# Resident expert weights in a macaron of attention, RWKV and four expert mixtures: per-tile weight transfers replaced by on-chip copies and register-addressed products

## What is computed

```
# glu stage (gated)
gate_logits = x @ Wg + bg
top_vals, top_idx = top_k(gate_logits, 2);  w = softmax(top_vals)
h = einsum('td,edh->eth', xf, W0) + b0          # d = 128, h = 512
g = silu(einsum('td,edh->eth', xf, W1) + b1)
y = einsum('eth,ehd->etd', h * g, W2) + b2
out = sum over the two chosen experts of w * y
# mlp stage (ungated): gelu(x @ W1 + b1) @ W2 + b2 for the two chosen,
# plus a shared gelu(x @ shared_W + shared_b), a layer norm, and the residual
```

## Time and profile before

| | |
|---|---|
| runs, median (lowest to highest) | 1119.5 us (1117.77 to 1120.09), 3 runs |
| profiled execution | 1118.18 us, its span 1116.4 us |
| TensorE busy | 797.7 us (71% of the span), 5220 matmul records |
| VectorE, ScalarE, GpSimd busy | 538.7, 445.3, 433.3 us (48%, 40%, 39%) |
| chain that ended last | PE 58%, DVE 24%, issue 7%, DMA 4%, ACT 3%, POOL 3% |
| DMA traffic | 153.77 MB, mean 138 GB/s |

### The profile page before, as it was taken

How to read it: one execution, slowest core, us unless ns; L and a number is a source line. 1 busy time by engine, 2 the same in 40 slices (tenths; PEclk the granted TensorE clock), 3 DMA queues, 4 the chain that set the end, 5 groups by cost and what they waited for, 6 DMA issues and landing times.

```text
span 1116.4 us, 17251 instructions
## 1 busy us (share of the span) xinstructions
PE 797.7 (71%) x5220; PEld 680.7 (61%) x5220; DVE 538.7 (48%) x1633; ACT 445.3 (40%) x1259; POOL 433.3 (39%) x448
## 2 busy tenths in 40 slices
PE   0579997378989865899974767774177877777750
PEld 0479997267777645798973566664034555666650
DVE  4734444777656537344447521113889543310117
ACT  0045554144445320455550145553087331265540
POOL 1256663022222210565631066663453210466631
PEclk9999999698989985799995579997598885699995
DMA  4559985362513003598954247775000011477752
GB/s 110 131 177 293 291 271 180 95 152 55 124 42 82 2 9 121 179 291 279 276 174 132 94 114 213 211 207 144 1 0 1 1 30 35 136 212 211 210 162 65
DMA packets 79082, 153.77 MB, mean 138 GB/s; under 512 B 11082, under 2 KB 54035, under 8 KB 78992
## 3 DMA queue, kind: packets, MB, share of 16 engines
q1 hardware_dynamic: 69008, 134.03, 40.6%
q0 software_dynamic: 9984, 18.65, 6.1%
HBM read 134.21 MB, written 20.25 MB: 138 GB/s over the span
## 4 chain that ended last, share of the span: by engine, by line
PE 58%; DVE 24%; issue 7%; DMA 4%; ACT 3%; POOL 3%; SPq 1%; another core or an unknown queue 0%; POOLq 0%; ACTq 0%; DVEq 0%
PE bank L521 14%; PE bank L512 12%; PE bank L509 8%; PE bank L945 2%; DVE stats L281 2%; PE bank L528 2%; PE bank L460 2%; PE bank L935 2%; DVE oh_b L623 2%; PE bank L497 2%; DVE sh_tok L675 2%; PE bank L1270 2%; DVE x_tok L675 2%; PE bank L908 1%; PE bank L477 1%
## 5 line engine op out<-in xcount | busy, mean ns | idle before, releaser
L512 PE MATMUL bank<-xt,weights 128*128 128x128 f32 x1248 | 249.8, 283 | 27.5 <-ACT xt L411 16.6
L521 PE MATMUL bank<-hid,weights 128*128 128x128 f32 x1248 | 245.1, 279 | 11.0 <-ACT hid L422 8.2
L348 POOL DMA_INDIRECT xg<-xn_rows,gidx x156 | 153.1, 982 | 238.7 <-DVE gidx L629 129.9
L512 PEld LDWEIGHTS bank<-xt,weights 128*128 128x128 f32 x1248 | 196.5, 199 | 33.9 <-ACT xt L411 20.3
L521 PEld LDWEIGHTS bank<-hid,weights 128*128 128x128 f32 x1248 | 191.1, 194 | 15.3 <-ACT hid L422 9.5
L355 POOL DMA_INDIRECT y_rows<-yo,sidx x156 | 157.1, 1007 | 91.8 <-issue 56.3
L650 DVE SCALAR_TENSOR_TENSOR hid<-bank,weights,act_ring 128x128 f32<-128x128 f32 x312 | 108.9, 349 | 139.5 <-ACT act_ring L422 83.2
L422 ACT ACTIVATE act_ring<-bank,weights 128x128 f32<-128x128 f32 x312 | 115.8, 371 | 111.1 <-PE bank L512 96.5
L657 DVE COPY yo<-bank 128x128 f32<-128x128 f32 x156 | 44.6, 286 | 213.2 <-remote 127.6
L422 ACT ACTIVATE hid<-bank,weights 128x128 f32<-128x128 f32 x312 | 110.6, 372 | 79.8 <-PE bank L521 51.1
L509 PE MATMUL bank<-xt,weights 128*128 128x128 f32 x624 | 128.8, 289 | 5.8 <-issue 2.5
(11 more groups left out here) (220 smaller groups left out, 1341.8 us busy)
## 6 DMA issues: line engine op xcount, KB each, us to landing
weights<-glu_pack SPq DMA_DIRECT2D x78, 772.5 KB
weights<-mlp_pack SPq DMA_DIRECT2D x78, 514.5 KB
v_sb<-v_rows SPq DMA_DIRECT2D x48, 180.0 KB, 6.5
y_in<-y_rows SPq DMA_DIRECT2D x32, 256.0 KB, 5.0
xn_rows<-xm_tok SPq DMA_DIRECT2D x16, 256.0 KB, 2.2
v_rows<-vd SPq DMA_DIRECT2D x16, 256.0 KB, 2.8
xg<-xn_rows,gidx POOLq DMA_INDIRECT x156
y_rows<-yo,sidx POOLq DMA_INDIRECT x156
```

The costliest lines, as they stand in the source:

```text
L348: pool.indirect_dma_start(out=xg[:, slot, :], out_offset=None, in_=xn_dram.ap()[:, :], in_offset=bass.IndirectOffsetOnAxis(ap=gidx[:, j:j ...
L512: nc.tensor.matmul(banks[k % 4][:, 0:TS], wt[:, slot, o:o + P], xt[:, j % 2, :], start=True, stop=True).then_inc(sem(st + "_up"), 1)
L521: nc.tensor.matmul(YD[j % 2], wt[:, j % WSLOTS, o:o + P], hid[:, k % 4, :], start=c == 0, stop=c == HC - 1).then_inc(sem(st + "_dn"), 1)
```

## The change

All eight experts' weights of a stage are brought into SBUF once, in `all_w`, by three transfers that are issued right after the normalised rows are written, in place of 39 transfers by tile. The packs are laid out as up weights, biases, down weights. VectorE copies the up weights and their biases of each tile from `all_w` to one of 4 slots of `wt`, three tiles ahead (two copies of 512 and 520 columns gated, one of 516 ungated). The down product swaps its operands: `hid` is stationary and the resident down weights move, addressed by a register, so the result is rows by features and needs no transpose. The ScalarE step `yt`, TensorE's output transpose and VectorE's copy are replaced by one VectorE add of the output bias, read from `out_bias` by register. `out_bias` is made once a stage: VectorE multiplies the identity by the eight bias columns (`diag`), TensorE multiplies a matrix of ones by it in two products of 512 columns, ScalarE copies both results to SBUF. The experts of eight tiles are packed into one integer, so that TensorE and VectorE load five words a stage and take three bits per tile by shift and mask.

```
-WSLOTS, XSLOTS, PIECES, LAG = 5, 6, 4, 3
+WSLOTS, XSLOTS, PIECES, LAG = 4, 6, 4, 3
+PACK = 8
+WORDS = -(-NTILE // PACK)
...
-        def tile_weights(sp, n, st, m, j):
-            slot = j % WSLOTS
-            pack = glu_pack if m.gated else mlp_pack
-            if j >= WSLOTS:
-                sp.wait_ge(sem(st + "_ysb"), st.at("_ysb", j - WSLOTS + 1))
-            e = sp.value_load(te_i[0:1, j:j + 1], min_val=0, max_val=E - 1)
-            sp.dma_start(wt[:, slot, 0:m.cols], pack[:, bass.ds(e * m.cols, m.cols)]).then_inc(
-                sem(st + f"_w_in{slot}"), 16)
+        def all_weights(sp, n, st, m):
+            pack = (glu_pack if m.gated else mlp_pack).rearrange("p (e c) -> p e c", e=E)
+            here = all_w[:, 0:E * m.cols].rearrange("p (e c) -> p e c", e=E)
+            up = m.ups * 512
+            for first, there, count in ((up, up + 512, m.down - up), (0, 0, up), (m.down, up, 512)):
+                sp.dma_start(here[:, :, first:first + count], pack[:, :, there:there + count]).then_inc(
+                    sem(st + "_weights_in"), 16)
+        def tile_words(eng, st, which=range(WORDS)):
+            eng.wait_ge(sem(st + "_te"), st.at("_te", 1))
+            return [eng.value_load(te_i[0:1, i:i + 1], min_val=0, max_val=E ** PACK - 1) for i in which]
+        def expert(words, j):
+            return (words[j // PACK] >> (3 * (j % PACK))) & (E - 1)
...
@@ moe_act
-            def tile_out(j):
-                act.wait_ge(sem(st + "_dn"), st.at("_dn", HC * (j + 1)))
-                if j >= 2:
-                    act.wait_ge(sem(st + "_yT"), st.at("_yT", j - 1))
-                act.activation(yt[:, j % 2, :], YD[j % 2], ACT.Identity,
-                               bias=wt[:, j % WSLOTS, m.bias_out:m.bias_out + 1]).then_inc(sem(st + "_ysb"), 1)
+            act.wait_ge(sem(st + "_rows"), st.at("_rows", 1))
+            for i in range(2):
+                act.activation(out_bias[:, 512 * i:512 * i + 512], BIAS[i][:, :], ACT.Copy).then_inc(
+                    sem(st + "_out_bias"), 1)
...
@@ moe_pe
+            words, first = tile_words(pe, st), [0, 0]
...
+            pe.wait_ge(sem(st + "_diag"), st.at("_diag", 1))
+            if not m.gated:
+                pe.wait_ge(sem(st + "_shared_act"), st.at("_shared_act", NBLK))
+            for i in range(2):
+                ins = nc.tensor.matmul(BIAS[i][:, :], ones_sq[:, :],
+                                       diag[:, 4 * i:4 * i + 4, :].rearrange("p e d -> p (e d)"), start=True, stop=True)
+            ins.then_inc(sem(st + "_rows"), 1)
...
-                    pe.wait_ge(sem(st + f"_w_in{slot}"), st.at(f"_w_in{slot}", 16 * (j // WSLOTS + 1)))
+                    pe.wait_ge(sem(st + "_tile_w"), st.at("_tile_w", j + 1))
...
-                    pe.wait_ge(sem(st + "_ysb"), st.at("_ysb", j - 1))
-                o = m.ups * 512 + c * P
-                nc.tensor.matmul(YD[j % 2], wt[:, j % WSLOTS, o:o + P], hid[:, k % 4, :],
+                    pe.wait_ge(sem(st + "_yo"), st.at("_yo", j - 1))
+                if c == 0:
+                    first[j % 2] = pe.snap(expert(words, j) * m.cols + m.down)
+                nc.tensor.matmul(YD[j % 2], hid[:, k % 4, :], all_w[:, bass.ds(first[j % 2] + c * P, P)],
                                  start=c == 0, stop=c == HC - 1).then_inc(sem(st + "_dn"), 1)
-            def tile_out(j):
-                pe.wait_ge(sem(st + "_ysb"), st.at("_ysb", j + 1))
-                if j:
-                    pe.wait_ge(sem(st + "_yo"), st.at("_yo", j))
-                nc.tensor.transpose(YO, yt[:, j % 2, :], ident[:, :]).then_inc(sem(st + "_yT"), 1)
...
@@ moe_dve, routing
-            nc.vector.tensor_scalar_min(te_i[0:1, :], te_f[0:1, :], E - 1.0).then_inc(sem(st + "_te"), 1)
+            nc.vector.scalar_tensor_tensor(digits, digits, E - 1.0, digit[0:1, :, :], ALU.min, ALU.mult)
...
+            nc.vector.tensor_reduce(te_word[0:1, :], digits, AX.X, ALU.add)
...
+            nc.vector.tensor_copy(te_i[0:1, :], te_word[0:1, :]).then_inc(sem(st + "_te"), 1)
...
+            words = tile_words(v, st, range(1))
+            v.wait_ge(sem(st + "_weights_in"), st.at("_weights_in", 16 * 3))
+            nc.vector.tensor_tensor(diag, ident[:, :].unsqueeze(1).broadcast_to(spread), biases.broadcast_to(spread),
+                                    ALU.mult).then_inc(sem(st + "_diag"), 1)
             v.wait_ge(sem(st + "_table"), st.at("_table", 1))
...
@@ moe_dve, tile loop
+            def tile_weights(j):
+                slot = j % WSLOTS
+                if j >= WSLOTS:
+                    v.wait_ge(sem(st + "_hid"), st.at("_hid", HC * (j - WSLOTS + 1)))
+                first = v.snap(expert(words, j) * m.cols)
+                for i in range(m.ups):
+                    lo, hi = 512 * i, m.bias_out if i == m.ups - 1 else 512 * (i + 1)
+                    ins = nc.vector.tensor_copy(wt[:, slot, lo:hi], all_w[:, bass.ds(first + lo, hi - lo)])
+                    if i < m.ups - 1:
+                        yield
+                ins.then_inc(sem(st + "_tile_w"), 1)
+                yield
             def tile_out(j):
-                v.wait_ge(sem(st + "_yT"), st.at("_yT", j + 1))
-                nc.vector.tensor_copy(yo[:, j, :], YO).then_inc(sem(st + "_yo"), 1)
+                v.wait_ge(sem(st + "_dn"), st.at("_dn", HC * (j + 1)))
+                nc.vector.tensor_tensor(yo[:, j, :], YD[j % 2], out_bias[:, bass.ds(expert(words, j) * D, D)],
+                                        ALU.add).then_inc(sem(st + "_yo"), 1)
+            for j in range(WSLOTS - 1):
+                for _ in tile_weights(j):
+                    pass
+            words += tile_words(v, st, range(1, WORDS))
+            v.wait_ge(sem(st + "_out_bias"), st.at("_out_bias", 2))
             for j in range(NTILE):
+                ahead = tile_weights(j + WSLOTS - 1) if j + WSLOTS - 1 < NTILE else iter(())
                 for c in range(HC):
                     chunk(j, c)
-                    if c == 1 and j >= 2:
-                        tile_out(j - 2)
+                    if c == HC - 1 and j:
+                        tile_out(j - 1)
+                    if c in (0, 2):
+                        next(ahead, None)
```

52 lines of the change are left out of this document (26 added, 26 removed).

## The result

The changed kernel took 1121.5 us (median of 12 runs, 1116.1 to 1127.1) and the kernel before, beside it on the same chip, 1117.6 us (12 runs, 1114.3 to 1120.1): a ratio of 1.0045, 95% interval 1.0029 to 1.0062. It is slower by some 4 to 5 us, where 1110 was forecast. The profiled execution of after took 1119.1 us (span 1116.6), among the faster of its twelve.

What follows compares the result with a forecast made beforehand. GpSimd's two indirect transfers a tile, making TensorE's signals late, were taken as the bound. Gated minus 5.3, ungated plus 2, tails minus 6, starts plus 3.4 gave minus 6, rounded to minus 8: 1118.2 to 1110 us, range 1068 to 1136.

Steps and rivals of the forecast that it cites:

- Rival one: Tile loops: late signals depend on traffic or signal count and go; about 1061 us, half effect 1088; chance 0.22.
- With the add a tile earlier the gap should be 0.30: minus 0.17.: Gated tile, GpSimd's gap between gather and scatter: falls from 0.47 to 0.30 us, saving 0.17 a tile.
- minus 5.3: Both gated loops: tile falls from 3.18 to 3.10 us, 0.08 x 33 tiles x 2.
- minus 0.06 us a tile: GpSimd's gather and scatter: without per-tile weight transfers both get shorter, together 0.06 us a tile.
- Copies, plus 0.15 gated: VectorE's two up-weight copies per gated tile lengthen GpSimd's operations by 0.15 us; ungated 0.1.
- Rival two: Tile loops: copies hold GpSimd up; 1135 us at 0.2 us each, 1177 at the full 0.41; chance 0.20.
- Tails, minus 6: Last tiles and end of each stage, without output transpose and copy: 1.5 us saved in each of four stages.
- Starts, plus 3.4: Stage starts: two small VectorE operations, 0.4 x 4, and gathers meeting copies, 0.9 x 2, add 3.4 us.
- Registers priced at nothing: TensorE's register work for down products in the loop: taken as 0, bound 0.3 us a gated tile.
- Rival three: Gated tiles: register work opens bubbles on TensorE, tiles take 3.37 us; 1128 us; chance 0.10.
- Ungated, plus 2: Ungated loops: a pair goes from 6.19 to 6.25 us, plus 1 us a stage, 2 in all.
- The single-tile rhythm: Ungated loops: one TensorE signal less may give a single-tile period of 3.05 us; total rounded from minus 6 to minus 8.

Runs made afterwards that it cites:

- experiment 13: Changed kernel with result rows written by SyncE's plain transfers in place of GpSimd's scatter, on the first kind of chip: 1016.8 us (kernel before 1110.7).
- 14: Changed kernel with both gather and scatter replaced by SyncE's plain transfers, on the first kind of chip: 996.7 us (kernel before 1110.7).
- experiment 15: Changed kernel with the next tile's transposition issued at the head of the tile on TensorE, first kind of chip: 1111.4 us (kernel before 1111.5).
- experiment 16: Changed kernel with TensorE's word loads behind the bias products and ungated tiles' copies on ScalarE, first kind of chip: 1110.4 us, ratio 1.0006.
- experiment 5: The changed kernel as it is, on the second kind of chip, beside the kernel before: 1046.3 us, ratio 0.9946.
- 9: Changed kernel with TensorE's five word loads moved behind the two bias products, second kind of chip: 1045.1 us, ratio 0.9941.
- experiment 10: Changed kernel with down products at a fixed address, no words or registers on TensorE, second kind of chip: 1045.1 us, ratio 0.9938.
- experiment 7: Kernel before plus only the transposed down product; weights still streamed per tile, no copies, second kind of chip: 1048.9 us, ratio 0.9973.

## Why the prediction was wrong

*The bound, and where it holds.* That GpSimd's dense indirect transfers make TensorE's signals late and set the tile was right for the chip of the result: experiments 13 and 14 take the transfers away on a chip of that kind and the lateness goes with them. Rival one (the late signals depend on traffic or on the number of signals) falls there: the traffic fell from 248 to 38 GB/s and the waits stayed. That the signals "come when it pauses" was too strong: in the first gated loop of after (tiles 6 to 30) 11 of the 35 results that ScalarE and VectorE read over 0.4 us late are read in the middle of a transfer (109.69 above). What one trace could not tell is that five of the eight chips show no lateness at all.

*The step that failed: "With the add a tile earlier the gap should be 0.30: minus 0.17."* The gap did become 0.30. But the working took the rest of the loop as fixed ("0.40 more until the late signal is seen"). It is not: the pause grew by 0.15. Gap and pause together stay where they are, 1.20 us before and 1.19 after, and on the chip of experiments 15 and 16 1.14 and 1.13, again with the gap at 0.47 in one and at 0.30 in the other. Why the sum stays is open. A circle of nearly the same length lies in after, transposition (112.27), late signal, xt (113.67), two chunks of up and down products, next transposition (115.45), 3.18 us; but experiment 15 cuts it and keeps the period of experiment 16, so it is not what holds the tile, or not alone. The term was 0.17 x 66 = 11 us; with 4 us for the traffic and 10 for the copies against it, it made the minus 5.3. What was measured in the gated loops is plus 0.5 (table, third line).

*Weight traffic, "minus 0.06 us a tile"* (for an ungated pair the sum has 0.14 where two tiles make 0.12). Zero: gathers stay at 0.97 and scatters at 1.01 without it. The 0.94 of the earlier trace rows belongs to gathers with no scatter about: experiment 13, gathers alone, has a median of 0.94 in every stage.

*Copies, plus 0.15 gated.* On the chip of the result nothing in the gated loops: gathers and scatters keep their length to 0.01 us and the copy itself grows to 0.61 to 0.70; in the ungated ones scatters go from 1.02 to a mean of 1.06 and 1.04 (tiles 6 to 30). On the second kind 0.12 and 0.07 a transfer, about what was taken, and hidden by 0.02 us. Which of the two grows goes by who starts first and by how much, on either kind of chip: where a copy starts 0.1 to 0.3 us ahead of a transfer, the transfer takes 1.09 us on average and the copy its 0.42 (25 pairs in after, 129 in experiment 5); where it starts 0.5 to 0.7 us into one, the transfer takes 1.00 and the copy 0.65 (108 pairs in after); a copy that starts 0.3 to 0.5 us into a transfer leaves both as they are (1.01 and 0.43). The prediction had placed the second copy on a scatter and expected nothing there. Rival two had the mechanism and not the price: at twice the copies GpSimd's loop is only 2.88. The rule of the Trainium skill weighed there (page SBUF — State Buffer, "Who interferes with whom", the later one blocks fully) is borne out only in part: it is the later one that grows, the transfer by 0.12 us and the copy by 0.2 to 0.3, but a copy that starts 0.4 us into a transfer keeps its 0.43 us while the transfer, at 1.01, goes on. With ScalarE's copies no lengthening is seen in the trace.

*Tails, minus 6.* The period behind the last gather did go from 2.90 to 2.79 and the parts behind the last transposition gained 3.0 us together; with six shorter tiles in the gated stages, 1.3 us, some 4.3. Over-sized, the right sign.

*Starts, plus 3.4.* Up to the first tile plus 3.1, but not from the terms named: the two small VectorE operations and the bias products were priced, and TensorE's loads of the words ahead of the table were not priced at all. They cost 2.2 us in the first stage (experiments 9 and 10 bring 2.0 of it back). The first tiles of the gated stages then lost 0.5 and 1.5 us, with the longest wait at 4.14 us for 2.40 and at 3.29 for 1.98; the ungated ones gained 0.4 together. The earlier rise of the clock was hidden, as the prediction said, and partly lost again: it is back at 0.50 in the window from 65.5 us.

*Registers priced at nothing:* right in the loop (experiment 10). Rival three is out.

*Ungated, plus 2:* plus 0.5 with the starts, small as forecast. The single-tile rhythm for which 2 us were taken off did not come. (Half of rival one's 57 us would be 1090, not 1088; nothing hangs on it.)

*Together.* Minus 5.3, plus 2, minus 6, plus 3.4 had been forecast; gated loops without their first tiles plus 0.5, ungated ones plus 0.9, starts plus 3.1 and plus 1.7, ends minus 3.0 were measured. The gated term alone would have kept the sign: with minus 5.3 in its place the sum is minus 2.7. What remains between the profiled plus 3.1 us in these stages and the medians' 3.9 was not taken apart; after's runs spread over 11 us, before's over 6. That the waits at the starts differ from run to run would explain it, but no run shows it.

*On the second kind* the change gains 5.7 us: 0.11 us of TensorE in each gated tile (minus 3.5 us a stage behind the first six intervals, 92.75 to 89.25 us) and shorter first six intervals (minus 2.9 and minus 2.5, though against a slow execution of the kernel before), and against them the loads (plus 2.5 up to the first tile) and the ungated stages (plus 1.3 and 0.9, mostly behind the last transposition). The 0.11 is the output transpose's worth, which the prediction set to nothing because GpSimd's loop was longer. Beyond that, resident weights beat streamed ones by 2.6 us (experiments 5 and 7), at the start of the second gated stage above all.

## What to carry to other kernels

A pause is not a constant. Before the shortening of one wait in a loop is booked as a gain, ask what ends the wait behind it: here 0.17 us less ahead of the scatter came back as 0.15 us more behind it, since the signal awaited there did not come earlier. Register and word loads are cheap in a loop and dear where work stands behind them in the engine's queue; try them where the engine waits for data anyway, and look at every stage whether the idle time they open leaves the clock down: moved behind the bias products they gained 2.5 us in one stage and lost 2.4 in the next. And run both kernels on more than one chip before trusting a difference of half a per cent: here its sign depends on the chip.

## What the runs showed of the hardware

- Two kinds of chips: with the same instructions and nearly the same length of each, the kernel before takes 1107 to 1120 us on one kind (two of seven, and that of the result) and 1049 to 1058 us on the other. The difference lies in the four tile loops: 468 us together in the trace of the kernel before on the first kind, 401 on the second, of spans of 1116 and 1055.
- On the first kind, while GpSimd runs two indirect transfers a tile (or gathers back to back), many of TensorE's signals are seen late by the other engines, by ScalarE 0.4 to 1.2 us late in the gated loops of after, up to 3.4 us at a loop's start (the product ended at 69.1 us, ScalarE starts at 72.46). Some are seen on time, within 0.04 us of the product's modelled end, and some late ones in the middle of a transfer. With one transfer a tile and a pause of 1.85 or 0.95 us this is gone behind the first tiles (but for one spot in four loops), and with none altogether. Why only these chips do it stays open.
- A load of one word from SBUF by TensorE takes 0.31 us (median of 20), the longest 1.97, and what stands behind it in the queue waits: the five of the first stage end at 52.1 us, 2.8 us after the first one-hots are there, and the table starts at 52.45.
- VectorE's 512-column copies beside GpSimd's indirect transfers: a copy that starts 0.1 to 0.3 us ahead makes the transfer 1.09 us (0.97 to 1.02 without one), one that starts 0.5 to 0.7 us into it grows itself, 0.42 to 0.65. In the gated loops that is the first case on the second kind (experiment 5) and the second case on the chip of the result. ScalarE's 516-column copy (0.63 us) leaves the transfers at 0.98 and 1.02.
- Weight transfers that fill the DMA engines delay a gather's rows: 6.1 us from the gather's start to the transposition of its rows with the engines busy 0.99 of the time (experiment 7), 2.8 us with 0.06 (experiment 5).
